# Two chained cross-attentions: inputs read in a second, transposed layout, the value bias as an extra matmul, normalisation on ScalarE, residuals stored in halves

## The chip, the cores and the metric

One core of one Trainium2 chip runs the whole program. The metric is the device time of one execution in microseconds. The kernel before takes 721.43 us (median of 3 runs, 720.66 to 721.87).

## The reference

x is 32 x 256 x 512 and ctx_512 is 32 x 256 x 256, all in float32. Two cross-attentions follow each other, for each of the 32 sequences (the calls with other sizes in the code only draw the weights):

```
# attention 0: softmax over the QUERIES (axis 1), then residual and layer norm
q = x @ Wq + bq;  k = ctx @ Wk + bk;  v = ctx @ Wv + bv
w = softmax(q @ k.T / sqrt(512), axis=1)
y = w @ v + x
x1 = (y - mean(y)) * rsqrt(var(y) + 1e-6) * gamma + beta

# attention 1: softmax over the KEYS, output projection, residual
Q = x1 @ Wq' + bq';  K = ctx @ Wk' + bk';  V = ctx @ Wv' + bv'
out = x1 + (softmax(Q @ K.T / sqrt(512), axis=-1) @ V) @ Wo' + bo'
```

The rows of w in attention 0 do not sum to 1, since the softmax is over the other axis. So the bias bv of v adds (row sum of w) x bv to y, and this row sum has to be computed.

## The kernel before

**Algebra.** The program folds the weights first: WQK = Wq Wk^T for each attention (512 x 256), WVO = Wv' Wo', and vectors for all that the biases add. The query side is then projected straight to the width of ctx: Y = x WQK, scores = Y ctx^T plus a term for each row.

**Precision.** Each operand is a pair of float32r tensors, `_hi` (rounded by ScalarE) and `_lo` (what rounding left: source minus hi). A product is three passes: hi hi, hi lo, lo hi (`passes`, L378). So each operand X that TensorE produces costs one ScalarE rounding from the PSUM bank (`round_bank`, L626) and one VectorE subtraction, called a cut here (`low`, L795, its instruction is L803 or, with a bias, L801).

**Tiling.** Two sequences form a pair: 512 query rows in J = 4 blocks of 128. There are 16 pairs. Iteration n does the front of pair n (attention 0) and the back of pair n-1 (attention 1), interleaved. The first iteration has only a front (and all weight preparation), a loop on the engines runs 7 times over two iterations, then come the last with a front (`before_last`) and one with only a back (`last`).

**Order.** It is written out by hand. Every engine has its own instruction queue and waits on semaphores; PSUM bank use is a fixed list (`STEADY`, L46) that gives each tile its bank, and `filled`/`emptied` counters of each bank. TensorE's iteration (L571) is: 16 transposes of x and 8 of ctx (`transpose_inputs`, L466), Y projection, transposes of n (the normalised rows of the pair before), spread of the row term r0, scores 0, Y1 projection, first half of WC = w ctx, row sums (L549), second half, scores 1, blocks pr 0 and 1 of the attention 0 output (`apply`, L560), transposes of the probabilities pt (8), pr 2, PC half 0, pr 3, PC half 1, and the four output blocks out 0 to 3.

**VectorE** (L1078): cuts of xT and cT, r0s (L921), cut of Y, cuts of nT, maxima 0, w_lo (L971, four of 128x256, both inputs in SBUF), cuts of Y1, four products of the row-sum bank with the identity that leave one row sum for each row (L1113), cuts of WC, r1s (L946), maxima 1 (L953), then additions, statistics, normalisations (L1007) and outputs (L980).

**GpSimd** (L1216): cut of ctx rows (`cn_lo`, L1146), products of n with u (L1185, two and two), four scalings n x gamma (L1207), the sum of the low halves of w (L1190, waits for w_lo), beta adds (L1214), bias adds to x (L1198), products of the next x with u (L1170) and rstd (L1177).

**ScalarE** (L729): all roundings, both exponentials, four bias rows bv x row sum (L710), and sums of GpSimd's products (L716, L726).

**SyncE** issues all DMAs: x and ctx of the next pair (L341, L346) and the store of a finished pair, 1 MB from R, behind its four outputs (L347 to L350).

The diff touches nearly every part, so these functions follow.

## Time and profile before

| what | value |
|---|---|
| median of 3 runs | 721.43 us |
| profiled execution, its own time | 719.84 us |
| its span, first to last instruction | 717.8 us |
| TensorE busy | 687.4 us, 96% |
| VectorE busy | 597.1 us, 83% |
| GpSimd busy | 489.5 us, 68% |
| ScalarE busy | 426.6 us, 59% |
| granted TensorE clock, mean | 0.993 |
| HBM read and written | 32.51 and 16.78 MB |

Busy time is an average over stages. What a change is worth is read from the stage that it touches: which wait ends last there. In the rows, PE is TensorE, DVE is VectorE, ACT is ScalarE, POOL is GpSimd, and a text in brackets is idle time of that engine just before the instruction, with what ended it. Buffer names have no numbers: u_b is u0_b or u1_b, bank is any PSUM bank.

### The profile page before, as it was taken

The page shows a single profiled execution, that of the slowest core. Times are in us where ns is not written, and L with a number is a line of the kernel's source. Part 1 is how long each engine was busy: PE and PEld are TensorE (multiplying, and loading weights), DVE is VectorE, ACT ScalarE, POOL GpSimd, SP SyncE. Part 2 cuts the span into 40 slices and gives each one's busy share as a digit, 9 for nine tenths or more (in the row PEclk, how much of TensorE's full clock was granted, in tenths as well). Part 3 has the DMA queues.
Part 4 walks back from the last instruction along what each step waited for, and adds up shares of the span by engine and source line. Part 5 has one row for each costly group of instructions (what it writes and reads, how often), then busy time and mean ns, then how long its engine had stood idle before and what let it go on. Part 6 is the DMA issues. An engine that isn't in the chain of part 4 may idle for free.

```text
span 717.8 us, 12706 instructions
## 1 busy us (share of the span) xinstructions
PE 687.4 (96%) x4107; PEld 596.5 (83%) x4107; DVE 597.1 (83%) x1362; ACT 426.6 (59%) x1009; POOL 489.5 (68%) x391
## 2 busy tenths in 40 slices
PE   8997999999999999999999999999999999999987
PEld 6875978988797898879788887978888798888876
DVE  4898698897979789797978879797887979798865
ACT  2644747657484765748476574847557484756632
POOL 0177776948486795848678584858868485886753
PEclk9998999999999999999999999999999999999999
DMA  8802004040210404021040403004040300301003
GB/s 287 299 1 64 25 1 147 2 146 0 79 67 0 146 0 146 0 95 51 0 146 0 146 0 114 32 7 139 0 146 0 126 21 25 121 0 59 1 0 118
DMA packets 30336, 49.50 MB, mean 69 GB/s; under 512 B 2160, under 2 KB 10352, under 8 KB 30320
## 3 DMA queue, kind: packets, MB, share of 16 engines
q1 hardware_dynamic: 30320, 49.29, 20.5%
q8 instruction: 9, 0.15, 0.1%
q14 instruction: 7, 0.06, 0.0%
HBM read 32.51 MB, written 16.78 MB: 69 GB/s over the span
## 4 chain that ended last, share of the span: by engine, by line
PE 74%; DVE 19%; issue 3%; POOL 3%; DMA 1%; ACT 1%; SPq 0%; DVEq 0%; POOLq 0%
PE bank L385 61%; PE bank L392 12%; DVE n L1007 6%; DVE stats L996 3%; DVE pc_lo L803 2%; DVE var_eps L1003 2%; DVE x_odd L991 1%; DVE x_even L991 1%; PE bank L405 1%; POOL x_even L1198 1%; DMA wk_sb<-in_L_xattn_Wk_dram 1%; DVE rb L918 1%; DVE n L827 1%; POOL wq_sb L1158 1%; POOL wq_sb L1154 1%
## 5 line engine op out<-in xcount | busy, mean ns | idle before, releaser
L1185 POOL TENSOR_TENSOR prod<-n,u_b 128x512 f32<-128x512 f32 x64 | 81.6, 1296 | 5.9 <-ACT prod L716 5.9
L801 DVE SCALAR_TENSOR_TENSOR y_lo<-bank,terms,y_hi 128x512 fp32r<-128x512 f32 x64 | 45.6, 749 | 37.1 <-ACT y_hi L630 37.1
L1214 POOL TENSOR_TENSOR r<-r,beta_b 128x512 f32<-128x512 f32 x60 | 76.3, 1300 | 0.0
L1207 POOL TENSOR_TENSOR r<-n,gamma_b 128x512 f32<-128x512 f32 x60 | 75.6, 1288 | 0.0
L632 ACT ACTIVATE xT_hi<-bank 128x512 fp32r<-128x512 f32 x64 | 33.0, 605 | 70.5 <-PE bank L392 70.5
L630 ACT ACTIVATE y_hi<-bank,terms 128x512 fp32r<-128x512 f32 x64 | 42.0, 679 | 52.0 <-PE bank L385 51.9
L385 PE MATMUL bank<-wvo_hi,pc_hi 128*128 128x512 f32 x128 | 52.2, 408 | 15.8 <-DVE pc_lo L803 15.8
L1177 POOL TENSOR_TENSOR rstd<-var_eps,minus_half 128x2 f32<-128x2 f32 x32 | 22.3, 697 | 62.1 <-DVE var_eps L1003 60.5
L726 ACT ACTIVATE e<-e 128x512 f32<-128x512 f32 x60 | 37.8, 630 | 35.6 <-POOL e L1170 35.0
L1146 POOL TENSOR_TENSOR cn_even_lo<-ctxn,cn_even_hi 128x1024 fp32r<-128x1024 f32 x8 | 19.2, 2395 | 56.6 <-ACT cn_even_hi L740 56.6
L385 PE MATMUL bank<-xT_hi,wqk_hi 128*128 128x512 f32 x128 | 52.8, 412 | 1.1 <-DVE xT_lo L803 1.1
L385 PE MATMUL bank<-wv_hi,wc_hi 128*128 128x512 f32 x128 | 52.0, 407 | 0.6 <-issue 0.6
L385 PE MATMUL bank<-xT_lo,wqk_hi 128*128 128x512 f32 x128 | 51.4, 402 | 0.0
L385 PE MATMUL bank<-xT_hi,wqk_lo 128*128 128x512 f32 x128 | 51.2, 400 | 0.0
L385 PE MATMUL bank<-wvo_lo,pc_hi 128*128 128x512 f32 x128 | 50.5, 395 | 0.0
L385 PE MATMUL bank<-wvo_hi,pc_lo 128*128 128x512 f32 x128 | 50.5, 395 | 0.0
L385 PE MATMUL bank<-wv_lo,wc_hi 128*128 128x512 f32 x128 | 50.5, 395 | 0.0
L385 PE MATMUL bank<-wv_hi,wc_lo 128*128 128x512 f32 x128 | 50.5, 395 | 0.0
L385 PE MATMUL bank<-nT_hi,wqk_lo 128*128 128x512 f32 x128 | 50.3, 393 | 0.0
L385 PE MATMUL bank<-nT_hi,wqk_hi 128*128 128x512 f32 x128 | 50.2, 392 | 0.0
L385 PE MATMUL bank<-nT_lo,wqk_hi 128*128 128x512 f32 x128 | 49.9, 390 | 0.0
L1190 POOL TENSOR_TENSOR y_lo<-w_lo 128x512 fp32r<-128x512 f32 x16 | 21.1, 1317 | 39.6 <-DVE w_lo L971 39.6
(198 smaller groups left out, 2475.6 us busy)
## 6 DMA issues: line engine op xcount, KB each, us to landing
out_dram<-r SPq DMA_DIRECT2D x15, 1024.0 KB, 5.0
x_even<-in_x_dram SPq DMA_DIRECT2D x8, 1024.0 KB, 7.5
ctxn<-in_ctx_dram SPq DMA_DIRECT2D x16, 512.0 KB, 4.0
x_odd<-in_x_dram SPq DMA_DIRECT2D x8, 1024.0 KB, 7.0
wq_sb<-in_L_xattn_Wq_dram SPq DMA_DIRECT2D x4, 256.0 KB, 3.7
wk_sb<-in_L_xattn_Wk_dram SPq DMA_DIRECT2D x2, 512.0 KB, 7.3
wv_sb<-in_L_xattn_Wv_dram SPq DMA_DIRECT2D x2, 512.0 KB, 9.4
wq_sb<-in_L_xattn_Wq_dram SPq DMA_DIRECT2D x1, 1024.0 KB, 11.3
```

Source lines behind the costliest of these rows:

```text
L385: mm = pe.matmul(dst, w, m, start=first and n == 0, stop=last and n == len(terms) - 1)
L392: mm = pe.transpose(dst[:, n * P:(n + 1) * P], src, ident[:])
L630: i = act.activation(dst, at((name, k))[:], ACT.Identity, bias=bias)
L632: i = act.activation(dst, at((name, k))[:], ACT.Copy)
L726: act.activation(x_prod[j % 2], x_prod[j % 2], ACT.Copy, accum_out=r0[:, j:j + 1]).then_inc(r0_ready, 1)
L801: i = dve.scalar_tensor_tensor(dst, src, bias, high.bitcast(F32), ALU.add, ALU.subtract)
L996: dve.bn_stats(stats[:, j, :], xn[:, j, :]).then_inc(stats_ready, 1)
L1007: dve.tensor_scalar(N[:, j, :], xn[:, j, :], mv[:, j, 0:1], rstd[:, j:j + 1], ALU.subtract, ALU.mult).then_inc(n_ready, 1)
L1177: pool.tensor_tensor(rstd[:, q], var_eps[:, q], minus_half[:, q], ALU.pow).then_inc(rstd_ready, 1)
L1185: pool.tensor_tensor(prod[j % 2][:], N[:, j, :], u_b[1][:], ALU.mult).then_inc(prod_ready, 1)
L1207: pool.tensor_tensor(r[:, j, :], N[:, j, :], gamma_b[:], ALU.mult).then_inc(scaled_ready, 1)
L1214: pool.tensor_tensor(r[:, j, :], r[:, j, :], beta_b[:], ALU.add).then_inc(resid_ready, 1)
```

## The change

What it does, part by part:

- The kernel reads x and ctx twice, once as rows and once in a layout with features on the partitions (`x_turned`, `ctx_turned`), and the weights Wq, Wk and Wv' transposed. All 24 transposes of a pair's inputs on TensorE go, and those of the weights. ScalarE rounds xT from SBUF in two instructions of 128x1024, VectorE cuts it in two; both now do this one pair ahead, around the WC roundings and cuts. ScalarE rounds cT in one instruction at the start of a pair, and GpSimd cuts it, ahead of the cut of ctx rows. `c_raw` shares its memory with E1.
- The row sums are four matmuls (w hi and w lo, two each) and no longer need GpSimd's sum of w_lo. ScalarE rounds 96 rows of the bank, VectorE cuts 32 of them, and the bias is a seventh matmul of each pr block, with 96 rows (`rs_rows`, `bv_rows`). The bias rows (ScalarE), the diagonal products (VectorE) and the bias adds (GpSimd) go.
- The vectors of the bias terms are one-column matmuls (`term_columns`) and not VectorE products.
- ScalarE normalises: n = x * rstd + shift, shift = -mean * rstd, where VectorE makes -mean and ScalarE shift.
- ScalarE's row terms 2 and 3 move behind the second xT rounding. GpSimd does all four beta adds together.
- PSUM banks go round 0 to 6. Y1 shares Y's memory.
- R is stored in two halves, each when its two outputs are done, each with its own semaphore; a GpSimd scaling waits for its half.

```diff
@@ SyncE
-                    for j in range(J):
-                        sp.wait_ge(emptied[BANK["out", j]], out_made[j])
-                    sp.dma_start(rows_of(out_rows, finished), R[:]).then_inc(rows_in_or_stored, 16)
+                    sp.wait_ge(xT_lo, xT_cut)
+                    sp.dma_start(x_raw[:], whole_pair(x_turned, pair_after)).then_inc(x_raw_loaded, 16)
+                    sp.wait_ge(cn_lo, pair_after)
+                    sp.dma_start(ctxn[:], rows_of(ctx_rows, upcoming)).then_inc(ctx_loaded, 16)
+                    sp.wait_ge(cT_lo, pair_after)
+                    if it.back:
+                        sp.wait_ge(filled[BANK["pt", 1]], pt_made)
+                    sp.dma_start(c_raw, whole_pair(ctx_turned, pair_after)).then_inc(c_raw_loaded, 16)
+                    for b in range(2):
+                        for j in range(b * RT, (b + 1) * RT):
+                            sp.wait_ge(emptied[BANK["out", j]], out_made[j])
+                        store_half(b, finished[b])
@@ TensorE
-                pe.wait_ge(w_lo_added, it.times(1, 1))
+                pe.wait_ge(w_lo, it.times(2 * RM, 2 * RM))
                 dst = begin(it, "rs")
-                end(product(dst[:], [(ones_r[:], W[0][:, :, mt, :]) for mt in range(RM)] + [(ones_r[:], w_lo_sum)]),
-                    "rs")
+                end(product(dst[:], [(ones_r[:], w[:, :, mt, :]) for w in W for mt in range(RM)]), "rs")
...
+                if name == "pr":
+                    if j == 0:
+                        wait_emptied(pe, it, "rs")
+                    terms.append((rs_rows[:BV_ROWS, j * P:(j + 1) * P], bv_rows[:BV_ROWS]))
...
-                    transpose_inputs(it)
                     project(it, "y", "xT", WQK[0], XT)
@@ ScalarE
+            def round_row_sums(it):
+
+                wait_filled(act, it, "rs")
+                act.activation(rs_rows[:BV_ROWS], at(("rs", 0))[:BV_ROWS], ACT.Copy).then_inc(hi["rs"], 1)
+
+            def normalise(it, j):
+
+                if j % RT == 0:
+                    act.wait_ge(mean_ready, it.times(2, j // RT + 1))
+                    act.wait_ge(rstd_ready, it.times(2, j // RT + 1))
+                    for n in range(j, j + RT):
+                        act.activation(shift[:, n:n + 1], minus_mean[:, n:n + 1], ACT.Copy,
+                                       scale=rstd[:, n:n + 1]).then_inc(shift_ready, 1)
...
+                act.activation(N[:, j, :], XN[it.parity][:, j, :], ACT.Identity, bias=shift[:, j:j + 1],
+                               scale=rstd[:, j:j + 1]).then_inc(n_ready, 1)
...
-                    row_terms(it, (2, 3))
                     for c in range(KC):
                         round_bank(it, "y1", c, Y1[0][:, c, :], bias=ccol[1][:, c:c + 1])
+                if more:
+                    round_xT(it, 0, 1)
+                if it.front:
+                    round_bank(it, "wc", 0, halves(WC[0], 0))
+                    round_row_sums(it)
+                    round_bank(it, "wc", 1, halves(WC[0], 1))
+                if more:
+                    round_xT(it, 1, 1)
+                if it.back:
+                    row_terms(it, (2, 3))
@@ VectorE
+            def cut_xT(it, h, ahead):
+
+                dve.wait_ge(hi["xT"], it.times(2, 2 * ahead + h + 1))
+                dve.tensor_tensor(XT[1][:, 2 * h:2 * h + 2, :], x_raw[:, 2 * h:2 * h + 2, :],
+                                  XT[0][:, 2 * h:2 * h + 2, :].bitcast(F32), ALU.subtract).then_inc(xT_lo, 1)
@@ GpSimd
+            def cut_cT(it):
+                pool.wait_ge(hi["cT"], it.times(1, 1))
+                pool.tensor_tensor(CT[it.parity][1][:], c_raw, CT[it.parity][0][:].bitcast(F32), ALU.subtract)\
+                    .then_inc(cT_lo, 1)
...
                 if it.front:
+                    cut_cT(it)
                     cut_ctx(it)
...
-                if it.front:
-                    add_w_lo(it)
-                if it.back:
-                    add_beta(it, (0, 1))
+                    add_beta(it, range(J))
...
-                if it.front:
-                    add_bias(it)
-                if it.back:
-                    add_beta(it, (2, 3))
                 more = it.j is not None or it.known < PAIRS - 1
                 if more:
                     x_products(it, (0, 1))
```

VectorE in the loop of the kernel before, from the cuts of the low half of w to the maxima of attention 1 (the register instructions between them and three repeats of the diagonal product are left out; e is E0 or E1, top the maxima):

```order
L971 SCALAR_TENSOR_TENSOR w_lo<-e,rinv,w_hi 128x256 x4
...
L801 SCALAR_TENSOR_TENSOR y_lo<-bank,terms,y_hi 128x512
...
L1113 ISA e,rs<-bank,ident 128x128
L1113 ISA rs 128x1
...
L803 TENSOR_TENSOR wc_lo<-bank,wc_hi 128x512 x2
L946 TENSOR_SCALAR r1s<-r,terms 128x4
...
L953 TENSOR_SCALAR e,top<-bank,r1s 128x256 x2
L960 TENSOR_SCALAR neg<-top 128x2
```

The same place in the kernel after:

```order
L966 SCALAR_TENSOR_TENSOR w_lo<-e,rinv,w_hi 128x256
...
L817 SCALAR_TENSOR_TENSOR y_lo<-bank,terms,y_hi 128x512
...
L852 TENSOR_TENSOR xT_lo<-x_raw,xT_hi 128x1024
L819 TENSOR_TENSOR wc_lo<-bank,wc_hi 128x512
...
L1086 TENSOR_TENSOR rs_rows<-bank,rs_rows 32x512
L819 TENSOR_TENSOR wc_lo<-bank,wc_hi 128x512
...
L852 TENSOR_TENSOR xT_lo<-x_raw,xT_hi 128x1024
L941 TENSOR_SCALAR r1s<-r,terms 128x4
```

Two cuts of 128x1024 with both inputs in SBUF now stand ahead of r1s, and the diagonal products are gone.

GpSimd in the loop of the kernel before, one pair, from its first instruction to the x products:

```order
L1146 TENSOR_TENSOR cn_even_lo<-ctxn,cn_even_hi 128x1024
L1185 TENSOR_TENSOR prod<-n,u_b 128x512 x2
...
L1207 TENSOR_TENSOR r<-n,gamma_b 128x512 x4
L1185 TENSOR_TENSOR prod<-n,u_b 128x512 x2
...
L1190 TENSOR_TENSOR y_lo<-w_lo 128x512
L1214 TENSOR_TENSOR r<-r,beta_b 128x512 x2
L1198 TENSOR_TENSOR x_even<-prod,x_even 128x512 x2
```

and in the kernel after (e in the first row is c_raw, which lies in E1):

```order
L1129 TENSOR_TENSOR cT_odd_lo<-e,cT_odd_hi 128x1024
L1124 TENSOR_TENSOR cn_odd_lo<-ctxn,cn_odd_hi 128x1024
...
L1167 TENSOR_TENSOR prod<-n,u_b 128x512
...
L1176 TENSOR_TENSOR r<-n,gamma_b 128x512 x2
...
L1167 TENSOR_TENSOR prod<-n,u_b 128x512 x2
L1183 TENSOR_TENSOR r<-r,beta_b 128x512 x4
...
L1152 TENSOR_TENSOR e<-x_even,u_b 128x512 x2
```

One more cut stands at the head, and the instruction that waited for w_lo (L1190) is gone: behind products 2 and 3 the beta adds follow at once.

## Rows read from the trace of the kernel before

**Rows 1.** The page, busy time: us, share of the span, instructions.

```profile
PE 687.4 (96%) x4107; PEld 596.5 (83%) x4107; DVE 597.1 (83%) x1362; ACT 426.6 (59%) x1009; POOL 489.5 (68%) x391
```

**Rows 2.** Windows of one pair: stretch, length, busy PE PEld DVE ACT POOL, clock, DMA.

```profile
276.29:292.56 16.27, 16.27 (x96) 14.09 (x93) 12.99 (x30) 12.37 (x32) 12.57 (x10) 1.00 0.48 156
292.56:301.83 9.27, 9.27 (x64) 8.52 (x63) 7.25 (x25) 6.73 (x16) 8.79 (x8) 1.00 0.00 0
301.83:315.35 13.52, 12.41 (x69) 10.35 (x68) 12.96 (x25) 4.95 (x12) 8.95 (x8) 1.00 0.00 0
315.35:317.89 2.54, 2.54 (x25) 2.54 (x24) 2.46 (x6) 1.90 (x4) 0.00 (x0) 1.00 0.07 27
```

**Rows 3.** Timeline of TensorE in this pair: start, us, instruction, idle before.

```profile
294.00 0.63 PE L385 MATMUL bank<-w_hi,ones_r 128*128 128x512 f32 x2
294.70 0.28 PE L385 MATMUL bank<-w_hi,cn_even_hi 128*128 128x256 f32 x1
...
312.45 0.50 PE L385 MATMUL bank<-wvo_hi,pc_hi 128*128 128x512 f32 x1 [1.11 <-DVE pc_lo L803]
```

**Rows 4.** Waits of TensorE, 100 to 640 us: total, times, longest.

```profile
PE bank L385 <- DVE pc_lo L803: 14.7, 13, 1.2
```

**Rows 5.** Timeline of GpSimd in this pair.

```profile
278.44 2.40 POOL L1146 TENSOR_TENSOR cn_even_lo<-ctxn,cn_even_hi 128x1024 fp32r<-128x1024 f32 x1 [5.21 <-ACT cn_even_hi L740]
280.80 2.53 POOL L1185 TENSOR_TENSOR prod<-n,u_b 128x512 f32<-128x512 f32 x2
283.29 5.04 POOL L1207 TENSOR_TENSOR r<-n,gamma_b 128x512 f32<-128x512 f32 x4
...
292.41 1.29 POOL L1190 TENSOR_TENSOR y_lo<-w_lo 128x512 fp32r<-128x512 f32 x1 [1.55 <-DVE w_lo L971]
...
314.15 0.69 POOL L1177 TENSOR_TENSOR rstd<-var_eps,minus_half 128x2 f32<-128x2 f32 x1 [3.96 <-DVE var_eps L1003]
```

**Rows 6.** Line 971: all w_lo cuts (ns min/median/max), and those of this pair.

```profile
L971 DVE SCALAR_TENSOR_TENSOR w_lo<-e,rinv,w_hi x64: 468/474/1225, 37.0 to 666.3; 128x256 fp32r<-128x256 f32 x64
...
289.91 2.41 DVE L971 SCALAR_TENSOR_TENSOR w_lo<-e,rinv,w_hi 128x256 fp32r<-128x256 f32 x4 [0.23 <-ACT w_hi L695]
```

**Rows 7.** Timeline of VectorE in the prologue.

```profile
49.17 1.77 DVE L827 CUSTOM_DVE_ANT_0 n<-wk_sb,bq_b 128x512 f32<-128x512 f32 x1
...
50.87 1.75 DVE L827 CUSTOM_DVE_ANT_0 n<-bk_b,bq_b 128x512 f32<-128x512 f32 x1
```

**Rows 8.** Timeline of GpSimd in the prologue.

```profile
50.34 3.39 POOL L1198 TENSOR_TENSOR x_even<-prod,x_even 128x512 f32<-128x512 f32 x2
```

**Rows 9.** Groups of VectorE: busy us, mean ns, idle before.

```profile
L803 DVE TENSOR_TENSOR wc_lo<-bank,wc_hi 128x512 fp32r<-128x512 f32 x32 | 22.0, 689 | 10.7 <-ACT wc_hi L632 10.7
...
L870 DVE TENSOR_TENSOR wv_lo<-wv_sb,wv_hi 128x1024 fp32r<-128x1024 f32 x1 | 1.2, 1218 | 0.0
```

**Rows 10.** Group of GpSimd: the scalings that wait for the store.

```profile
L1207 POOL TENSOR_TENSOR r<-n,gamma_b 128x512 f32<-128x512 f32 x60 | 75.6, 1288 | 0.0
```

**Rows 11.** Groups of ScalarE.

```profile
L710 ACT ACTIVATE prod<-bv_b,rs 128x512 f32<-128x512 f32 x32 | 23.0, 719 | 17.4 <-DVE rs L1113 17.4
...
L740 ACT ACTIVATE cn_odd_hi<-ctxn 128x1024 fp32r<-128x1024 f32 x8 | 8.8, 1104 | 0.0
```

**Rows 12.** Timeline of VectorE and ScalarE: r1s, and the last exponential.

```profile
297.72 0.28 DVE L946 TENSOR_SCALAR r1s<-r,terms 128x4 f32<-128x4 f32 x1
...
301.04 0.50 ACT L703 ACTIVATE e<-e,neg 128x256 f32<-128x256 f32 x1
```

**Rows 13.** Timeline of TensorE between pair 0 and pair 1.

```profile
61.00 1.09 PE L392 MATMUL bank<-ident,x_odd 128*128 128x128 f32 x8 [1.09 <-DVE x_even L991]
63.53 1.97 PE L392 MATMUL bank<-ident,ctxn 128*128 128x128 f32 x8 [1.44 <-DVE beta_b L902]
66.63 0.77 PE L385 MATMUL bank<-xT_hi,wqk_hi 128*128 128x512 f32 x1 [1.13 <-DVE xT_lo L803]
```

**Rows 14.** Window 60 to 68 us, columns as in rows 2.

```profile
60.00:68.00 8.00, 4.43 (x19) 3.60 (x20) 7.68 (x15) 6.20 (x15) 3.65 (x4) 0.71 0.22 67
```

More of the change, by code:

```diff
@@ L126, in fill, with two_cross_attentions @@
         return self.times(steady, first - steady + upto(STEADY, STEADY.index(tile) + 1))
[L129 to L130 removed]
+def two_cross_attentions(nc, x, ctx, x_turned, ctx_turned, wq0_turned, wk0_turned, wv0, wq1_turned, wk1_turned,
+                         wv1_turned, wo1, columns, bv0_rows, gamma, beta, bo1, out):
     S, T, D = x.shape
@@ L463, in prepare1c @@
                         dst = begin(it, "bo1")
-                        end(product(dst[:], [(ones_r[:].bitcast(F32), wq1_sb[:, 0, :])]), "bo1")
-            def transpose_inputs(it):
-                xn = XN[it.parity]
-                pe.wait_ge(x_loaded[it.parity], it.loads())
-                for k in range(KD):
-                    transposes(it, "xT", k, [xn[:, j, k * P:(k + 1) * P] for j in range(J)])
-                pe.wait_ge(ctx_loaded, it.times(16, 16))
-                for c in range(KC):
-                    transposes(it, "cT", c, [ctxn[:, j, c * P:(c + 1) * P] for j in range(J)])
+                        end(product(dst[:], [(ones_r[:].bitcast(F32), bv_wo_sb[:, 0, :])]), "bo1")
             def transpose_n(it):
@@ L1068, in norm_and_output @@
                     output(it, 2)
-                if it.front and not it.before_last:
-                    normalise(2)
-                    normalise(3)
                 if it.back and not it.before_last:
@@ L1079, in iteration @@
                 begin_it = it.j is None and it.known == 0
+                more = it.j is not None or it.known < PAIRS - 1
                 if begin_it:
```

426 lines of the change are left out of this document (192 added, 234 removed).

## The prediction

> **What bounds the kernel now.** I read the page's busy shares first: TensorE is busy for 96% of the span [rows 1]. Then I cut one pair of the steady loop into stages, from the first matmul of its Y projection (276.29, called t = 0 below) to that of the next (317.89): 41.60 us, granted clock 1.00 (2.4 GHz), TensorE busy in all of three stages and missing 1.11 us in the fourth [rows 2]. That 1.11 us is its only wait: the third output block waits for the low half of PC, which VectorE reaches late [rows 3]; the same wait has 13 entries and 14.7 us between 100 and 640 us [rows 4]. So a pair is TensorE's own work plus 1.1 us. The transposes of the inputs are the stage from 315.35 to 317.89, 2.54 us [rows 2].
>
> **TensorE's own work after the change.** Per pair the transposes go: -2.54. The wait before the third output goes if the low half of PC comes 1.2 us sooner (1.11 idle and a first matmul that is 0.1 slower [rows 3]): the two normalisations ahead of it leave VectorE, which is more than that, while ScalarE now does them between the two PC roundings; by 0.33 x 2 + 0.8 x 2 (below) that still ends in time. -1.2. The row sums take four matmuls instead of three: three take 294.00 to 294.70, so 0.23 each [rows 3]; +0.23. The bias is one more 512-column matmul for each of four blocks: +0.93. Together 41.60 - 2.54 - 1.2 + 0.23 + 0.93 = 39.0 us a pair, if nothing new ends late.
>
> **What the other engines get.** VectorE loses the cuts of xT and cT (6 of 0.69, like that of wc [rows 9]), four normalisations and the four diagonal sums, and gets two 128x1024 cuts (1.22 each with GpSimd idle [rows 9]), a row-sum cut and two small minus-mean instructions. ScalarE loses four bias rows (0.72 [rows 11]) and gets four normalisations and four 128x1 shifts. No row has a 128x1 activation: 0.72 is the upper bound, and the line through 1024 columns (1.10) and 512 (0.72) [rows 11] leaves 0.33 for none, which I take; below nothing is excluded, as they are added. GpSimd loses the w_lo sum and four bias adds (5 x 1.3) and gets the cut of cT (2.4, like that of ctxn [rows 5]). In sums all three are lighter or level, so totals say nothing; the order does.
>
> **GpSimd and VectorE take turns.** In the prologue VectorE has three products with both inputs in SBUF one behind the other while GpSimd has a backlog: two of them start 1.70 us apart and last 1.77 and 1.75 [rows 7], and two GpSimd adds in the same stretch need 3.39 [rows 8] where two take 2.5 elsewhere (280.80 to 283.29 [rows 5]). So the instruction behind waits for the whole one on the other engine, and after each the other engine gets its turn. In the loop of before this hardly costs: of four w_lo cuts the first meets the end of a GpSimd product (up to 1225 ns against a median of 474), and all four take 2.41 [rows 6], because GpSimd then stands 1.55 idle, waiting for w_lo itself [rows 5].
>
> The change takes that gap away. GpSimd's first work of a pair, now the cut of cT, starts when ScalarE is through its new work: rstd ends at 314.84 [rows 5], 0.5 before out's end, then two shifts (0.66), two normalisations (0.8 each: 0.72 and one operand more) and the rounding of cT (1.1 [rows 11]): t = 2.5. Before, the cut of ctxn started at 278.44, t = 2.15. With 2.36 more in front, everything behind is 2.7 later, and the sum that waited for w_lo is gone: two products to t = 9.7, four scalings to 14.7, products 2 and 3, four beta adds and two x products follow with no gap. The w_lo cuts are due at t = 13.6 (289.91). The first goes in at 14.7; each then waits for one GpSimd instruction, 1.25 and 0.25 for its own reading, so 1.5 apart (bounds 0.5, with no turns taken, and 1.7, as in the prologue): the second is done at 16.5, the fourth at 19.5. TensorE wants two at t = 16.3 (wait 0.2) and all four for the row sums at 17.9 (wait 1.6). **Added: 1.8.**
>
> VectorE then has two Y1 cuts (1.4, to 20.9), the first xT cut, three PSUM cuts (0.69, 0.62 apart: 1.85 [rows 9]), the second xT cut, and r1s. All GpSimd's instructions still queued are 1.25 long, and their ends stand at 20.75 and 22.0: the xT cut goes 22.0 to 23.1, the PSUM cuts end at 25.0, the second xT cut waits for an x product until 25.6 and ends at 26.7, and r1s waits for the last x product, done at 28.0 or so. Nothing like this stood there before: r1s began at 297.72 (t = 21.4), was done at 298.0, and the last exponential ended at 301.54, 3.5 later [rows 12]. Now 28.1 + 3.5 = 31.6. Queued behind r1s are all maxima of the second attention, ScalarE waits for those, and TensorE for its exponentials: it reaches the last four transposes of the probabilities at 25.9 + 1.8 + 0.7 = 28.4. **Added: 3.1** (0.4 if no turns were taken, since ScalarE's two row terms now stand behind the second xT rounding). A pair is 39.0 + 1.8 + 3.1 = 43.9; phases I can't read to 0.1 make it 43.3 to 44.3. I take 43.8, +2.2 against 41.6.
>
> That the xT cuts take turns is carried over from the w_lo cuts and the prologue's products; no row has a plain two-input SBUF subtraction against a busy GpSimd. The Trainium skill, SBUF — State Buffer, section Who interferes with whom, says that a tensor_tensor with both inputs in SBUF contends with a GpSimd instruction that reads SBUF and that the later one is blocked in full; it speaks against this change, and by it the sum is that of my forecast, without it that of the second rival.
>
> **The rest.** Half stores: a GpSimd scaling never waited for the store (idle before it 0.0 [rows 10]), so two semaphores win nothing; the added queue entry on SP stands behind output 1, where nobody waits. SP's new loads of turned x and ctx wait for the second xT cut (t = 26.7) and the last transpose (t = 32); the first user is the cut of cT at t = 46 and later, over 10 us behind them, so they cost nothing; with that cover gone a late load would hold the Y projection. The last front pair has no xT cuts and no x products: its w_lo waits stay (+1.8) and its own 2.5 goes, roughly +1 with what follows. Start: the weights' transposes go, 28 one-column matmuls come, TensorE stands idle for the first loads; between pair 0 and pair 1 the input transposes stand with three waits among them, up to 66.63, at a granted clock of 0.71 (the second eight start at 61.00 behind 1.09 idle, so by an estimate the first start 1.0 before that idle, at 58.9) [rows 13, 14], and go, while normalised rows now come later from ScalarE, which has roundings of WVO and four sums ahead of them. Of that 7.8 I keep 3 (bounds: -8, all of it, and +5, idle at the start and half clock behind it).
>
> **Sum.** 14 full pairs x 2.2 = +31, last front pair and tail +1.5, start -3: +29.5. From the profiled execution's own 719.84 that is 749.3. Its time is 1.6 under the median of the runs (721.43), so 750.
>
> **Rivals.**
> - *Nobody is late (faster).* The place is the same, VectorE's w_lo and xT cuts: if GpSimd doesn't get its turn between two VectorE instructions, w_lo is done by t = 16, r1s at 23.3, and only 0.4 at the probabilities' transposes is left. A pair is 39.4: 14 x -2.2 = -31, last pair -2.5, start -3: 683, range 678 to 700. For it: VectorE and GpSimd are lighter in sum. Against it: the prologue's 1.70 apart [rows 7]. It decides as soon as the w_lo cuts come under 0.9 us apart. Chance 0.20.
> - *Only half of it.* w_lo takes turns, the xT cuts don't: r1s at 19.5 + 1.4 + 1.1 + 1.85 + 1.1 = 25.0, exponentials done at 28.8, wait 0.4: 39.0 + 1.8 + 0.4 = 41.2, so -0.4 a pair: 14 x -0.4 = -6, and -1.5 for both ends: 714, range 700 to 728. Chance 0.14.
> - *The clock too.* Waits of 1.1 us a pair leave the granted clock at 1.00 [rows 2, 3], three of 1.1 to 1.4 in one stretch go with 0.71 and a first Y matmul of 0.77 [rows 13, 14]. With 4.9 us of waits a pair, some 5 us of it at 1.2 GHz would cost 2.5 more: 750 + 14 x 2.5 = 785. Chance 0.08.
> - *Forecast*: 0.58, own range 738 to 762.
>
> **Numbers.** A change of under 0.2% (1.4 us) can't be told from none. Faster: 0.20 and 0.09 of the half case, 0.29. Same 0.05. Slower 0.66. The range of 696 to 770 takes in the forecast, nearly all of the half case and the edges of the other two.
>
> **What would show it.** Right: in a pair, w_lo cuts 1.4 to 1.6 apart and GpSimd with no idle time from the cut of cT to the second x product; new TensorE waits of about 1.6 before the row sums (released by w_lo) and 3 at the probabilities' transposes (by ScalarE's exponential); no wait for the low half of PC; pairs of 43.8. Wrong: w_lo cuts 0.4 apart (first rival), xT cuts of 1.2 and not 1.8 to 2.3 (second), a granted clock under 1.00 in the loop (third). It also goes wrong if GpSimd starts its pair much sooner or later than t = 2.5, since this phase decides which instruction meets which.

## The result: 22% slower, over five times the loss that was forecast

| | before | after |
|---|---|---|
| median of 4 runs | 721.04 us | 882.29 us (881.51 to 882.95) |
| ratio, 95% interval | 1 | 1.2238 (1.2215 to 1.2261) |
| span of the profiled execution | 717.8 us | 880.0 us |
| granted TensorE clock, mean | 0.993 | 0.897 |

The direction was right, the size was not: 161 us and not 29. Where the span's 162.2 us lie is read from the first Y matmul of pair 1 and of the last front pair:

| stretch | before | after | difference | forecast |
|---|---|---|---|---|
| start, to Y of pair 1 | 66.6 | 91.0 | +24.4 | -3 |
| 14 pairs | 584.1 | 710.8 | +126.7 | +31 |
| last front pair and tail | 67.1 | 78.2 | +11.1 | +1.5 |

The page of the kernel after, busy shares, granted clock (in tenths, 40 slices of the span) and the costliest group (line, engine, operation, then busy us and mean ns):

```profile
PE 721.3 (82%) x3855; PEld 619.7 (70%) x3855; DVE 641.3 (73%) x1123; ACT 446.1 (51%) x1031; POOL 426.5 (48%) x327
...
PEclk9677999798997979899797989989797988979799
...
L935 DVE TENSOR_SCALAR neg<-mx 128x2 f32<-128x2 f32 x32 | 167.0, 5219 | 3.4
```

TensorE's share fell from 96% [rows 1] to 82%, and the largest group of VectorE is one that no step of the prediction named: the negation of two maxima, 256 numbers, with a mean of 5.2 us. Its line (ns min/median/max), of before and of after:

```profile
L940 DVE TENSOR_SCALAR neg<-mx x32: 170/204/499, 31.8 to 662.7; 128x2 f32<-128x2 f32 x32
```

```profile
L935 DVE TENSOR_SCALAR neg<-mx x32: 169/318/11631, 47.2 to 824.7; 128x2 f32<-128x2 f32 x32
```

There are two in a pair. In the kernel after, the first of them lasts 11.6 us in 14 of the 15 pairs behind pair 0. VectorE and GpSimd at that place of a steady pair:

```profile
303.47 0.08 DVE L927 DVE_READ_ACCUMULATOR2_ANT mx<- 128x1 f32 x1
303.65 11.62 DVE L935 TENSOR_SCALAR neg<-mx 128x2 f32<-128x2 f32 x1
315.19 0.41 DVE L927 CUSTOM_DVE_ANT_0 e<-bank,rb 128x256 f32<-128x256 f32 x1
```

```profile
302.78 5.12 POOL L1176 TENSOR_TENSOR r<-n,gamma_b 128x512 f32<-128x512 f32 x4
307.82 2.54 POOL L1167 TENSOR_TENSOR prod<-n,u_b 128x512 f32<-128x512 f32 x2
310.30 4.94 POOL L1183 TENSOR_TENSOR r<-r,beta_b 128x512 f32<-128x512 f32 x4
```

The negation is issued 0.87 into GpSimd's first scaling and ends when GpSimd's row does (310.30 + 4.94 = 315.24): nine GpSimd instructions start while it waits. I call that a lock-out. The row ends there because GpSimd's next instruction, the first product for the next pair, itself waits for w_lo (`x_products`), and w_lo stands in VectorE's queue behind the negation: GpSimd then stands 4.3 idle. What waits behind it is seen in the waits (total us, times, longest), in TensorE's timeline, and in the windows of the whole pair and of two stretches of it (columns as in [rows 2]):

```profile
ACT e L681 <- DVE neg L935: 169.4, 16, 11.7
...
PE bank L388 <- DVE w_lo L966: 130.8, 16, 9.2
```

```profile
318.75 0.58 PE L388 MATMUL bank<-w_hi,cn_odd_hi 128*128 128x256 f32 x1 [9.18 <-DVE w_lo L966]
```

```profile
295.00:346.10 51.10, 41.81 (x229) 36.18 (x229) 39.72 (x68) 27.54 (x65) 26.21 (x20) 0.90 0.23 82
305.00:313.00 8.00, 4.57 (x20) 3.35 (x18) 8.00 (x1) 0.00 (x0) 8.00 (x8) 1.00 0.00 0
318.00:331.00 13.00, 12.25 (x65) 11.33 (x66) 10.58 (x23) 8.20 (x19) 2.52 (x2) 0.74 0.00 0
```

ScalarE's exponentials wait 11.7 for the negation, w_lo comes behind them, TensorE stands idle for 9.2 until w_lo is there, and behind this idle time the granted clock is 0.74 over 13 us (part of it at 1.2 GHz). In the second window ScalarE does nothing at all. A pair of 51.1 us is then TensorE's own 39.2 (measured below in a kernel without the lock-out), 9.2 of wait, and 41.81 - 39.2 = 2.6 of the same matmuls at the lower clock: 51.0.

Where the forecast looked, VectorE and GpSimd did as it said in pair 1 only, the one of the 15 without a lock-out: there the negations last 1.21 and 0.47, the four w_lo cuts 5.17 (forecast 1.5 apart), the first xT cut 2.23. Its length is no test of the forecast, since it follows the start: 49.2 us here, 43.2 in the kernel before and 45.6 in experiment 7, where no such turns are left.

### The profile page after: what moved, and what is told of

Read it like the earlier page. It is cut to its first block, busy times and chain, and to the rows that moved or that the text cites. A ratio compares the mean times of both kernels' runs of the same rounds, so it can differ in the third digit from the quotient of the medians.

```text
span 880.0 us, 11830 instructions
## 1 busy us (share of the span) xinstructions
PE 721.3 (82%) x3855; PEld 619.7 (70%) x3855; DVE 641.3 (73%) x1123; ACT 446.1 (51%) x1031; POOL 426.5 (48%) x327
## 4 chain that ended last, share of the span: by engine, by line
PE 51%; DVE 31%; ACT 10%; issue 5%; POOL 1%; DMA 1%; SPq 0%; DVEq 0%; POOLq 0%; ACTq 0%
PE bank L388 46%; DVE neg L935 18%; DVE nT_lo L819 3%; ACT e L681 3%; ACT e L696 2%; PE bank L424 2%; PE bank L407 2%; DVE xT_lo L852 2%; DVE y_lo L817 2%; PE bank L395 2%; DVE e L948 1%; ACT w_hi L688 1%; ACT xT_hi L643 1%; ACT y_hi L621 1%; DVE w_lo L966 1%
## 5 line engine op out<-in xcount | busy, mean ns | idle before, releaser
L935 DVE TENSOR_SCALAR neg<-mx 128x2 f32<-128x2 f32 x32 | 167.0, 5219 | 3.4
L681 ACT ACTIVATE e<-e,neg 128x256 f32<-128x256 f32 x64 | 31.7, 496 | 169.4 <-DVE neg L935 169.4
L817 DVE SCALAR_TENSOR_TENSOR y_lo<-bank,terms,y_hi 128x512 fp32r<-128x512 f32 x64 | 45.6, 748 | 78.4 <-ACT y_hi L621 77.2
L388 PE MATMUL bank<-w_hi,cn_odd_hi 128*128 128x256 f32 x64 | 25.2, 394 | 65.3 <-DVE w_lo L966 65.3
L388 PE MATMUL bank<-w_hi,cn_even_hi 128*128 128x256 f32 x64 | 25.9, 405 | 64.3 <-DVE w_lo L966 64.3
L1152 POOL TENSOR_TENSOR e<-x_odd,u_b 128x512 f32<-128x512 f32 x32 | 40.8, 1288 | 58.4 <-DVE w_lo L966 39.3
L388 PEld LDWEIGHTS bank<-w_hi,cn_odd_hi 128*128 128x128 f32 x64 | 18.4, 288 | 69.6 <-DVE w_lo L966 68.8
L388 PEld LDWEIGHTS bank<-w_hi,cn_even_hi 128*128 128x128 f32 x64 | 18.9, 296 | 68.1 <-DVE w_lo L966 67.3
L852 DVE TENSOR_TENSOR xT_lo<-x_raw,xT_hi 128x1024 fp32r<-128x1024 f32 x32 | 51.5, 1613 | 20.5 <-ACT xT_hi L643 19.1
L975 DVE SCALAR_TENSOR_TENSOR r<-bank,rinv,r 128x512 f32<-128x512 f32 x60 | 45.1, 751 | 21.4 <-PE bank L388 21.3
L1152 POOL TENSOR_TENSOR e<-x_even,u_b 128x512 f32<-128x512 f32 x28 | 36.8, 1326 | 35.9 <-DVE w_lo L966 26.0
```

Of the source, the lines that this page charges most:

```text
L388: mm = pe.matmul(dst, w, m, start=first and n == 0, stop=last and n == len(terms) - 1)
L681: e = act.activation(E0[:, b, mt, :], E0[:, b, mt, :], ACT.Exp, bias=neg0[:, q:q + 1], accum_out=sum0[:, q:q + 1])
L817: i = dve.scalar_tensor_tensor(dst, src, bias, high.bitcast(F32), ALU.add, ALU.subtract)
L852: dve.tensor_tensor(XT[1][:, 2 * h:2 * h + 2, :], x_raw[:, 2 * h:2 * h + 2, :], XT[0][:, 2 * h:2 * h + 2, :].bitcast(F32), ALU.subtract).t ...
L935: dve.tensor_scalar(neg0[:, q], mx0[:, q], -1.0, None, ALU.mult).then_inc(neg0_ready, 1)
L975: dve.scalar_tensor_tensor(r[:, j, :], at((name, j))[:], rinv1[:, j:j + 1], r[:, j, :], ALU.mult, ALU.add).then_inc(emptied[BANK[name, j]], 1)
```

## The experiments

Theory A, after the traces: a VectorE instruction that shares SBUF access with GpSimd can be locked out until GpSimd's row ends, and everything else of the loss in the loop hangs on that. Theory B: the clock falls for its own reasons. Later, on A: is it the form of the instruction, its place, or a race? All ratios are to the kernel before, run beside it on the same chip.

### 1. The negations on ScalarE

```diff
@@ ScalarE, softmax0, ahead of the exponentials
+                    act.activation(neg0[:, q2], mx0[:, q2], ACT.Copy, scale=-1.0).then_inc(neg0_ready, 1)
@@ VectorE, maxima0
-                    dve.tensor_scalar(neg0[:, q], mx0[:, q], -1.0, None, ALU.mult).then_inc(neg0_ready, 1)
```

> The changed kernel, with the two negations of the layer-0 maxima (VectorE tensor_scalar, 128x2) made by ScalarE in front of its exponentials instead. Theory A, the lock-out: the 11.62 us that the first negation lasts in nearly every pair is VectorE waiting for a port of SBUF that GpSimd's back-to-back products hold, and everything in the pair after it, the fallen clock (0.74 in 318 to 331) too, follows from it. Then the exponentials come some 11 us earlier, TensorE's 9.18 us wait for w_lo falls to 1 to 3 us, the granted clock of a pair is 1.00, a pair costs 43 to 45 us instead of 51.1, and the kernel takes 765 to 800 us. Theory B, the clock: the clock falls for reasons of its own and the negation is a bystander; the pairs stay at 49 us or more and the time over 850 us. Theory C: the lock-out only moves to the next VectorE instruction that meets GpSimd's backlog (a cut of w_lo), then one of these takes 8 us or more and the time stays over 850 us.

Measured: 841.96 us, ratio 1.1695 (1.166 to 1.1729), pairs of 47.8. Line 966 of this kernel:

```profile
L966 DVE SCALAR_TENSOR_TENSOR w_lo<-e,rinv,w_hi x64: 470/473/9009, 50.6 to 787.9; 128x256 fp32r<-128x256 f32 x64
```

Theory C: the lock-out moved to the next VectorE instruction that reads two SBUF inputs, the first w_lo cut, 8.9 to 9.0 us in each of the 15 pairs behind pair 0. My 765 to 800 was wrong.

### 2. The negation with two SBUF inputs

```diff
-                    dve.tensor_scalar(neg0[:, q], mx0[:, q], -1.0, None, ALU.mult).then_inc(neg0_ready, 1)
+                    dve.scalar_tensor_tensor(neg0[:, q], mx0[:, q], 2.0, minus_half[:, q], ALU.mult, ALU.mult)\
+                       .then_inc(neg0_ready, 1)
```

> The changed kernel, with the two negations made by VectorE at the same place as a scalar_tensor_tensor, (maximum x 2) x minus_half, which reads two SBUF operands, instead of a tensor_scalar that reads one. Theory A1: only an instruction of the tensor_scalar kind (one source in SBUF, one destination in SBUF) is shut out while GpSimd works back to back, a form with two SBUF sources waits one GpSimd instruction at most; then no negation lasts over 1.4 us, pairs cost 43 to 46 us, and the kernel takes 765 to 810 us. Theory A2: any form that is issued at this place waits to the end of GpSimd's row of products; then the negation still lasts over 8 us and the time is 870 to 890 us.

Measured: 887.5 us, ratio 1.2322 (1.2291 to 1.2353).

```profile
L937 DVE SCALAR_TENSOR_TENSOR neg<-mx,minus_half x32: 160/685/11640, 43.7 to 829.8; 128x2 f32<-128x2 f32 x32
```

A2: with two SBUF inputs the negation is locked out just the same, in all 15 pairs.

### 3. A gap in GpSimd's row for the negations

```diff
@@ GpSimd, ahead of scale_n
+                        pool.wait_ge(neg0_ready, it.times(2, 2))
```

> The changed kernel, with GpSimd waiting for both negations before it scales N with gamma, so that there is nothing of GpSimd for them to meet. Lock-out theory: the negations last 0.2 us each, GpSimd stands idle 1 to 2 us a pair and its scalings and betas end that much later, in exchange for 11 us; pairs of 44 to 46 us and a time of 775 to 815 us. Clock theory: time over 850 us.

Measured: 783.33 us, ratio 1.0893 (1.085 to 1.0936), pairs of 44.38. The negations and the w_lo cuts, and the windows of a pair:

```profile
L935 DVE TENSOR_SCALAR neg<-mx x32: 169/169/1219, 44.3 to 724.5; 128x2 f32<-128x2 f32 x32
```

```profile
L966 DVE SCALAR_TENSOR_TENSOR w_lo<-e,rinv,w_hi x64: 481/1516/1533, 48.8 to 730.4; 128x256 fp32r<-128x256 f32 x64
```

```profile
268.81:313.20 44.39, 40.97 (x230) 34.77 (x229) 33.86 (x68) 27.88 (x65) 29.00 (x20) 0.96 0.26 94
```

One wait more, and the kernel is 99 us faster. Theory B falls. Here are the turns that I had forecast, 1.5 us at the w_lo cuts, and pairs of 44.4 against my 43.8 (GpSimd's gap of 2.45 is new in it). That the two times are so near is partly luck: I had 39.0 of TensorE's work and 4.9 of waits at the full clock, and the pair has 3.4 of waits (44.39 - 40.97) and 1.8 of slower matmuls (40.97 - 39.2). What it keeps of the loss is 42 in the 14 pairs (626.2 against 584.1), 20 at the start and 1 at the end.

### 4. The kernel before with a longer row

```diff
@@ GpSimd, cut_ctx of the kernel before: the cut is made twice
+                pool.tensor_tensor(CN[it.parity][1][:], ctxn[:], CN[it.parity][0][:].bitcast(F32), ALU.subtract)\
+                    .then_inc(cut_twice, 1)
+                pool.wait_ge(cut_twice, it.times(1, 1))
```

> The kernel before, with the low cut of the context rows on GpSimd made twice (2.4 us more work a pair at the start of GpSimd's row of products, as much as the changed kernel's cut of cT adds; same result). By the lock-out theory in its plain form (a GpSimd instruction that follows another at once never lets a tensor_scalar in) the first negation would have been shut out in the kernel before as well, where it lasts 0.26 us; so it must be chance or phase, and this run has either 0.2 to 1.3 us (turns) and a time of 720 to 735 us, or a first negation of over 5 us that lasts until GpSimd first waits, and a time of over 770 us. The clock theory has nothing to say of it: 720 to 735 us.

Measured: 750.1 us, ratio 1.0405 (1.0378 to 1.0433), pairs of 43.5 (+1.9), negations 169/194/1370 ns (min/median/max), no lock-out. The time lies between my two numbers: the row itself, 2.4 longer, costs 1.9 a pair by turns, since GpSimd's sum of w_lo and the w_lo cuts (median 1200 ns, 474 before [rows 6]) come later. A longer row alone doesn't bring a lock-out. The place isn't that of the kernel after, though: from pair 2 on the first negation is issued 1.1 into a scaling, as in the kernel before, and not 0.87.

### 5 and 6. The same row, some tenths of a microsecond later

```diff
@@ GpSimd, cut_cT: four instructions of 128x256 (in the other run two of 128x512) for one of 128x1024
+                for q in range(4):
+                    part = slice(q * 256, (q + 1) * 256)
+                    i = pool.tensor_tensor(lo[:, part], raw[:, part], high[:, part].bitcast(F32), ALU.subtract)
```

> The changed kernel with one thing moved in time only: GpSimd's low cut of cT is made as four instructions of 128x256 instead of one of 128x1024, so that all of GpSimd's row that follows starts some 0.3 to 0.5 us later against VectorE (estimate: the starts of four more-or-less fixed costs; row and work are the same). In the changed kernel the first negation is issued 0.83 to 0.88 us into a scaling in every steady pair and lasts 11.6 us. Race theory: whether VectorE gets the port at the next boundary of GpSimd or only when GpSimd's row ends is decided by when it asks, within some hundredths of a microsecond; issued at another point (about 0.4 to 0.6 us in) the negation gets its turn, lasts under 1.3 us, and the kernel takes 775 to 800 us, as the run with a gap did (783 us). Row theory: whoever comes first into a row of back-to-back GpSimd instructions waits for its end, at whatever point; then it lasts over 8 us and the time stays over 870 us.

> As the run before, with the cut of cT in two instructions of 128x512: GpSimd's row later by 0.1 to 0.2 us only, so the negation is issued some 0.65 to 0.8 us into the scaling. Race theory: if the window is as narrow as hundredths of a microsecond, the negation lasts under 1.3 us here too and the time is 775 to 800 us; if it is tenths wide, it is still shut out. Row theory: over 8 us and over 870 us.

Measured: 885.86 us (ratio 1.2296) and 884.8 us (1.2281). The negation is now issued 0.44 to 0.47, and 0.70 to 0.75, into a scaling, and in every pair from the second on lasts 12.0 and 11.7. So no window of hundredths or tenths around 0.87 does it; both my numbers for the race were wrong, the row theory was right for these two. But in pair 1 of both, the two negations at 0.86 to 1.22 get in within 1.4 us, and then the first w_lo cut is locked out for 9.5: place alone doesn't decide either way.

### 7. Out of each other's way

ScalarE makes both negations and r1s; GpSimd makes four row products first and scales N when w_lo is cut; VectorE's xT cuts come where GpSimd has little left.

```diff
@@ GpSimd
-                    row_products(it, (0, 1))
+                    row_products(it, range(J))
                     if it.front:
-                        scale_n(it)
-                if it.back:
-                    row_products(it, (2, 3))
-                    if not it.front:
-                        scale_n(it)
+                        pool.wait_ge(w_lo, it.times(2 * RM, 2 * RM))
+                    scale_n(it)
@@ VectorE: cut_xT(it, 0, 1) behind statistics(2), cut_xT(it, 1, 1) behind statistics(3)
@@ ScalarE, behind row_terms(2, 3); neg0 and neg1 as in experiment 1
+                    act.activation(r1s[:], r1[:], ACT.Identity, bias=ccol[1][:, KC:KC + 1]).then_inc(r1s_ready, 1)
```

> The changed kernel rearranged so that no VectorE instruction that works in SBUF alone meets GpSimd's row: both negations and the shift r1s are made by ScalarE, GpSimd makes its four row products first and scales N only when w_lo is cut, and the two cuts of xT are made 12 to 18 us later, in the stretch where GpSimd has only the products for the next pair. Theory (all of the excess of a steady pair over TensorE's own 39.0 us is VectorE and GpSimd meeting): pairs of 39.5 to 41 us against 51.1, and with the start of 86 to 91 us that these kernels have (66.6 before) a time of 710 to 735 us. Rival: a steady pair of the changed kernel has another bound of about 43 us (ScalarE's longer queue, 27.5 us busy of 51 and more here); then 755 us or more.

Measured: 721.1 us, ratio 1.0004 (0.9987 to 1.0022). Windows of two steady pairs:

```profile
254.00:294.08 40.08, 39.23 (x230) 33.82 (x229) 27.25 (x63) 28.52 (x70) 27.30 (x20) 1.00 0.29 105
334.10:374.17 40.07, 39.21 (x230) 33.78 (x229) 27.25 (x63) 28.52 (x71) 27.28 (x20) 1.00 0.30 105
```

Every arithmetic step of the change is still there, and 161 us are gone. The 14 pairs are now 17 us shorter than in the kernel before (566.9 against 584.1), and the start, 21.5 us later, takes that back. TensorE's own work is 39.2 (forecast 39.0), the clock 1.00. VectorE's busy time fell from 39.7 to 27.3 us a pair. The instructions that left VectorE are of 0.2 to 0.3 us, so nearly all of the 12.4 was waiting, which the page counts as busy.

### 8. The kernel before with half stores

```diff
@@ SyncE, kernel before
-                    sp.dma_start(rows_of(out_rows, finished), R[:]).then_inc(rows_in_or_stored, 16)
+                        store_half(b, finished[b])
```

> The kernel before with the stores of the residuals alone changed, to two halves with a semaphore each. The prediction costed this at nothing: 719 to 723 us, ratio 0.998 to 1.002. Rival: the earlier first half lets GpSimd scale earlier and shifts its row against VectorE, which could win or cost a microsecond a pair: 705 or 740 us.

Measured: 721.0 us, ratio 1.0015 (0.9981 to 1.0048), pairs of 41.6. No difference can be told, as costed.

### 9. The start mended as well

```diff
@@ TensorE, from the kernel of experiment 7; u, and in the same way the column terms
-            columns = ([(wqT[:, :, k * P:(k + 1) * P], bk_col[L]) for k in range(KD)] ...
-                        mm = pe.matmul(dst[:, n:n + 1], w[:, e, :], v[:, e:e + 1], start=e == 0, stop=e == KD - 1)
+                    mm = pe.matmul(dst[:], bk_col[L][:, e:e + 1].to_broadcast([P, P]), wqT[:, e, :],
+                                   start=e == 0, stop=e == KD - 1)
@@ SyncE: wk0 loaded ahead of wq0
@@ GpSimd, first iteration
+                        pool.wait_ge(r0s_ready, 1)
                     cut_cT(it)
```

> The kernel out_of_each_others_way with its start changed as well. In that kernel the first 88.2 us hold 28 + 28 fp32 matmuls of one column (10.0 and 7.2 us) and the granted clock is 0.64 right behind each set of them. Here the row u (128x512) is made as four matmuls with a broadcast column of bk as weights and 512 columns moving, in place of 16 of one column and four transposes, and the column terms as four matmuls 256 wide whose diagonal VectorE takes; the keys' weights are loaded first; and GpSimd cuts cT and cn only when VectorE's four dot products are done (they took 2.8 us each beside it, 0.7 alone). Theory (the start is late by the one-column matmuls, by the clock that they leave behind and by VectorE and GpSimd meeting): Y of the second pair starts at 68 to 77 us instead of 88.2, pairs stay at 40.1 us, and the time is 701 to 711 us, 1.5 to 3% under the kernel before. Rival: the start is bound by loads and by the chain of layer 1's weights, whatever TensorE does; then 717 us or more.

Measured: 708.67 us, ratio 0.9818 (0.9791 to 0.9846); Y of pair 1 starts at 75.58. It beats both kernels, the one before by 1.8%. The mean clock of the profiled execution is 0.997.

### 10 and 11. VectorE meeting GpSimd, and nothing else

The edit is a kernel of its own; its core, for VectorE against ten (then twelve) back-to-back GpSimd products of 128x512:

```
dve.memset(banks[5][:, :d], 0.0)                                # moves the meeting
dve.tensor_scalar(neg[:, 0], small[:, 0:2], -1.0, None, ALU.mult)
dve.scalar_tensor_tensor(w[:, k], e[:, k], small[:, 0:1], e[:, k], ALU.mult, ALU.subtract)
```

> Not the reference's computation, only VectorE meeting a row of GpSimd: GpSimd makes ten products of 128x512 in SBUF back to back; VectorE starts at the same signal, writes PSUM for some 3 us (a row of memsets), then makes a tensor_scalar of 128x2 in SBUF, a PSUM memset, a second tensor_scalar, another memset, and two scalar_tensor_tensors of 128x256. The first meeting is moved in six steps of about 0.1 us each, for three kinds of row: without waits, with a wait that is met on each product, and with each product waiting for the one before it; all three times over. Theory of a race at the boundary: some of the 54 meetings get their turn at the next boundary (under 1.3 us) and others are shut out until the row ends (5 to 10 us), and the same place of meeting can give either. Theory of order: the kind of row decides (a row whose instructions wait lets VectorE in, one without does not), the place does not. Theory that the lock-out needs more than these two engines (ScalarE or a DMA at work too): none of the 54 lasts over 1.4 us.

> Not the reference's computation. As m1_meetings, with twelve GpSimd products in a row, and nearer to the kernel: VectorE comes to the meeting out of three subtractions from PSUM into SBUF and a maximum with an accumulator, and in turn nobody else works, ScalarE makes activations in SBUF, TensorE makes matmuls, and both do; six places of meeting each, twice over (48 meetings). Theory that the lock-out needs a third engine at work: with ScalarE or TensorE some meetings last over 5 us and with neither none does. Theory that it needs VectorE to come out of its own SBUF writes: they last long in all four. If none of the 48 is over 1.4 us, what it takes is neither of these, and stays open.

Measured, first kernel (two tensor_scalars, then two scalar_tensor_tensors), then the second:

```profile
L89 DVE TENSOR_SCALAR neg<-small x54: 157/844/1193, 5.0 to 740.5; 128x2 f32<-128x2 f32 x54
...
L91 DVE TENSOR_SCALAR neg<-small x54: 749/833/954, 5.9 to 741.7; 128x2 f32<-128x2 f32 x54
...
L94 DVE SCALAR_TENSOR_TENSOR w<-e,small x108: 399/936/1474, 7.3 to 743.4; 128x256 f32<-128x256 f32 x108
```

```profile
L125 DVE TENSOR_SCALAR neg<-small x48: 169/316/1286, 8.1 to 739.0; 128x2 f32<-128x2 f32 x48
...
L128 DVE SCALAR_TENSOR_TENSOR w<-e,small x96: 1035/1302/1522, 8.8 to 741.6; 128x256 f32<-128x256 f32 x96
```

Of 360 meetings none lasts over 1.53 us: none waits for more than one GpSimd instruction (57 of the first kernel's, at 0.16 and 0.40 us, for none). In these small kernels neither the kind of row nor ScalarE or TensorE at work brings a lock-out, so what one needs is not in them. This is the rule that I had read from the prologue [rows 7], clean, and it is not what the kernel does.

### 12. The cut of cT on VectorE

```diff
@@ GpSimd
-                    cut_cT(it)
@@ VectorE, ahead of the cut of Y
+                    dve.tensor_tensor(CT[it.parity][1][:], c_raw, CT[it.parity][0][:].bitcast(F32), ALU.subtract)\
+                       .then_inc(cT_lo, 1)
```

> The changed kernel with one part of the change put elsewhere: the low cut of cT (128x1024) is made by VectorE, in the 4.8 us in which it waits for y_hi, and GpSimd's row is as it was before the change and starts 2.4 us earlier. If the lock-out came from the row's length or its new place (the cut of cT is what put it there), the first negation is let in as in the kernel before (0.2 to 1.3 us), pairs take 43 to 45 us and the kernel 765 to 800 us. If it can strike wherever VectorE meets the row, whatever its length, a negation or a w_lo still lasts over 5 us, a pair over 46 us and the kernel over 820 us.

Measured: two times, 826.83 and 844.91 us, against 721.58 for the kernel before: clearly slower, though not by one number. Only the execution of 844.91 us has a profile. Two pairs of it, VectorE, then GpSimd:

```profile
251.92 0.36 DVE L935 TENSOR_SCALAR neg<-mx 128x2 f32<-128x2 f32 x1
...
482.79 10.30 DVE L935 TENSOR_SCALAR neg<-mx 128x2 f32<-128x2 f32 x1
```

```profile
249.69 5.10 POOL L1174 TENSOR_TENSOR r<-n,gamma_b 128x512 f32<-128x512 f32 x4
...
480.56 5.12 POOL L1174 TENSOR_TENSOR r<-n,gamma_b 128x512 f32<-128x512 f32 x4
```

Both negations stand at the same place, 2.23 after the row of scalings began (0.96 into its second). One is let in at the next boundary, the other locked out for 10.3. Of the pairs 2 to 15, two go like the one at 251.92, and they take 42.0 us where the others take 48.3 to 49.8. In pair 1 the second negation is issued 0.89 into a scaling and locked out for 10.3; in the kernel after it is issued 0.88 in and takes 0.47. So I call it a race: by place the two cases can't be told apart. The row's place and length (back at what it was before the change) don't decide it.

DMA traffic is a rival that the change itself suggests, since it loads more: from pair 1 on no packet is under way at the negations of the kernel before, and 16 to 20 are at the first negation of pairs 2 to 14 in the kernel after. The traces speak against it both ways. In the last front pair of the kernel after, nothing is left to load, no packet is under way, and the negation at 812.31 is locked out for 11.6 all the same; the one at 251.92 above is let in at a DMA share of 0.85.

### 13 and 14. The start, edit by edit

The two runs are experiment 9 without its GpSimd wait, and experiment 7 with nothing but that wait.

> The kernel out_of_each_others_way (721.1 us) with the wide matmuls for u and the column terms and the keys' weights loaded first, but with GpSimd cutting cT and cn as soon as they are rounded: what start_mended (708.7 us) has, without its wait. The second pair's Y started at 88.2 us in the one and 75.6 in the other. If the one-column matmuls and the clock behind them are the larger part of the late start, this run keeps 8 us or more of the 12.4: under 713 us. If the meetings of VectorE's dot products with GpSimd are, it keeps under 5: over 716 us.

> The kernel out_of_each_others_way (721.1 us) with nothing but GpSimd waiting, in the first pair alone, for VectorE's r0s before it cuts cT and cn; the one-column matmuls stay. The four dot products and r0s then take some 3.5 us instead of 10.4, the spreading of r0s on TensorE waits 0 to 1 us instead of 4.7, unless the cuts (5.6 us) are late for the scores in their turn. If the one-column matmuls are the larger part of the late start, this gains under 5 us: over 716 us. If the meetings are, it gains over 7: under 714 us.

Measured: 715.97 us, ratio 0.9891 (0.9822 to 0.9959), Y of pair 1 at 81.5; and 716.62 us, ratio 0.9958 (0.9926 to 0.999), Y of pair 1 at 84.2. From 88.2, the wide matmuls with the load order win 6.6, the later cuts 3.9, together 12.6. These are single executions, and they scatter: the kernels after, of experiment 2 and of experiment 3 start alike, and their Y of pair 1 stands at 91.0, 86.4 and 86.5. So 12.6 is clear of that, and its shares are not. By the times of the runs the second has a gain of 4.5, under 5, and the first of 5.1, neither 8 nor under 5 (three of its four runs took 715.7 to 716.4 us, one 707.4). That the one-column matmuls are the larger part isn't shown. The one-column matmuls in the kernel after, their windows, and VectorE's dot products beside GpSimd in its start:

```profile
L424 PE MATMUL bank<-cols,wqT x64: 167/250/353, 18.6 to 58.4; 128*128 128x1 f32 x64
```

```profile
18.60:28.50 9.90, 9.73 (x57) 9.62 (x55) 0.89 (x3) 0.66 (x2) 0.00 (x0) 0.62 1.06 368
55.00:63.50 8.50, 8.50 (x58) 8.50 (x56) 1.23 (x1) 1.78 (x3) 1.80 (x2) 0.71 0.01 2
29.40:34.30 4.90, 4.90 (x14) 3.84 (x13) 3.68 (x5) 3.44 (x4) 2.81 (x2) 0.50 0.95 369
```

```profile
31.29 0.69 DVE L913 CUSTOM_DVE_ANT_0 rb<-x_even,u_b 128x512 f32<-128x512 f32 x1
...
32.02 2.77 DVE L913 CUSTOM_DVE_ANT_0 rb<-x_even,u_b 128x512 f32<-128x512 f32 x1
...
34.84 2.80 DVE L913 CUSTOM_DVE_ANT_0 rb<-x_even,u_b 128x512 f32<-128x512 f32 x1
...
37.68 3.44 DVE L916 TENSOR_SCALAR r0s<-r,terms 128x4 f32<-128x4 f32 x1
```

In the first two windows the weight loads (PEld) are busy nearly throughout, 9.62 of 9.90 and all of 8.50: a one-column matmul took what the load of its 128x128 weights took. The two sets, 28 matmuls or 56 records each, take 10 and 9 us, the clock granted in these windows is 0.62 and 0.71, and in the Y matmuls right behind the first set 0.50, the lower level. (In experiment 3, with the same start, the first set took 7.6.) And four dots of 0.69 become 10 us with r0s, since two of them and r0s each meet a long GpSimd instruction. The wide forms of experiment 9 are not short either: the first set takes 11.2 us (3.75, 1.71 and 5.78). But it starts at 5.5 and not at 18.6, while the other weights are still being loaded, and the clock in it and behind it, from 5.4 to 24.6, is 1.00.

## Why the prediction was wrong, point by point

- **TensorE's own work, 39.0 a pair: right.** 39.2 in experiment 7. The wait for the low half of PC is gone in the kernel after, as argued; in experiment 7 0.6 of it comes back.
- **GpSimd's start at t = 2.5, shifts of 0.33 and normalisations of 0.8: right.** It starts at t = 2.35, two shifts take 0.48 and two normalisations 1.51. My own terms, from 0.5 before t = 0, add up to 2.9 and not to 2.5; the nearer number was luck.
- **"After each the other engine gets its turn": the step that failed.** It holds in all 360 meetings of experiments 10 and 11, in pair 1, and in all steady pairs of experiment 3. In the kernel after it fails once in each pair from the second on, at the first negation, and the one wait is for nine instructions and not one: 11.6 us of VectorE, 9.2 of TensorE and 2.6 of slower clock, where I had 1.8 and 3.1. I had two contacts of the prologue [rows 7] for it. They couldn't show the other case, and I carried them over as a law. By the Trainium skill, page SBUF — State Buffer, section Who interferes with whom, the later of two such instructions is blocked for the whole of the other; a row of others isn't spoken of. Here the trace decides: it can be blocked for a row.
- **The negations were not in the sum at all.** I listed w_lo, the xT cuts and r1s as VectorE's contacts. The two negations stand ahead of them in the same row of GpSimd, and stood there before, among the scalings of [rows 5]:

```profile
286.85 0.26 DVE L940 TENSOR_SCALAR neg<-mx 128x2 f32<-128x2 f32 x1
```

  Of 0.2 us, they looked like nothing. A count of every VectorE instruction that falls in GpSimd's row would have had them first.
- **"W_lo waits add 1.8, the probabilities' transposes 3.1": right as a mechanism, where it can act.** Experiment 3 has turns of 1.5, and in a pair TensorE waits of 1.2 for w_lo and 2.1 for the exponentials, 3.4 where I had 4.9.
- **The clock as a rival at 785: the mechanism came.** In the kernel after it costs 2.6 us a pair, forecast 2.5, but behind one wait of 9.2 and not behind several short ones, so the near number is luck. In experiment 3, with waits of up to 1.9 and no lock-out, it costs 40.97 - 39.2 = 1.8: there the rival's mechanism acts by turns too, and my forecast had left it out. The other two rivals, nobody late and only half of it, both had no more than turns in them, as the forecast had; so no case that I gave a chance held a time over 800.
- **Half stores nothing, SyncE's loads nothing: right** (experiment 8, and 40.1 us pairs with all loads in place).
- **Start -3: wrong by 27.** I priced 28 one-column matmuls as if they were small, and there are two sets of 28. Each set costs 9 to 10 us of TensorE and the clock behind it, and the dots there meet GpSimd's new cuts. The upper bound of that term I had put at +5; it was +24. Some 13 of the 24 are shown by experiment 9. Experiment 7 starts 2.9 sooner (91.0 to 88.2), which is within the scatter of single executions; the rest, 9 to 12, I didn't take apart.
- **The sign to look for, "GpSimd with no idle time", was wrong.** I had written that nothing in the row waits for w_lo any more. The products for the next pair still do, and GpSimd stands 4.3 idle there in each steady pair, as w_lo is late.

What stays open is what makes a contact fall one way or the other. None of these decides it alone: the form (1, 2), the place in a GpSimd instruction (5, 6, 12), the row's length or place (4, 12), DMA traffic (12). A semaphore wait in the row, and a third engine at work, weren't enough to bring it on in the small kernels (10, 11); what they do in the kernel wasn't tried. The same place in the same kernel gives both. Keeping VectorE's SBUF instructions out of the row is the only cure shown.

## What to carry to other kernels

Count the VectorE instructions that touch GpSimd's row, down to the ones of 0.2 us, and price each with two numbers: one GpSimd instruction if it gets its turn, the whole rest of the row if not. If TensorE hangs behind it, take it out of the row, by giving it to ScalarE or by ordering the row around it; the same arithmetic was 161 us faster so. A matmul of one column isn't a small one: 28 of them took 7 to 10 us. The wide form gained here by its place and the clock, not by being shorter.

## What the runs showed of the hardware

- A VectorE instruction with its data in SBUF waited while 6 to 9 GpSimd instructions started (8.9 to 12.0 us), both as tensor_scalar and as scalar_tensor_tensor. GpSimd lost nothing meanwhile: nine instructions of 1.24 us pitch. In the rows shown the wait ended where GpSimd itself had to wait for VectorE.
- The same kernel can have it in some pairs and not in others (experiment 12). Its run times of 826.8 and 844.9 us would fit two or three pairs more let in, at 6.3 to 7.7 each; the faster run has no profile, so that isn't shown.
- Such a wait is counted as busy time. The page showed VectorE 73% busy, and 167 us of that were 32 negations.
